# Two-layer transformer on one core: reordering square sums, scatters and one shared product in the first layer

## The reference

```python
def step(state, inp):                 # attention of layer 0: a scan with rotation, 6 heads of 64
    th, ps, ph, vt, at, bt = inp
    retained = _rotate(state, ph) * at[..., None]
    write = _rotate(vt, ps)
    new_state = retained + bt[..., None] * write
    out_t = _rotate(new_state, -th)
    return (new_state, out_t)
...
rms = jax.lax.rsqrt(jnp.mean(jnp.square(out), axis=-1, keepdims=True) + EPS)
o = out * rms * rms_w * jax.nn.silu(g)
return o.reshape(B, T, VALUE_DIM) @ Wo
...
shared = _swiglu(x, wg_s, wu_s, wd_s) * RATIO        # FFN of layer 0: shared part, 16 experts, 2 a token
affinity = jax.nn.sigmoid(jnp.einsum('bsh,eh->bse', x, centroids))
_, top_idx = jax.lax.top_k(affinity + gate_bias, K)
...
for e in range(E):
    routed = routed + mask[..., e:e + 1] * _swiglu(x, wg[e], wu[e], wd[e])
return shared + routed
```

## Time and profile before

| | us |
|---|---|
| median of three runs | 2143.7 |
| lowest, highest | 2142.53, 2146.38 |
| the profiled execution | 2146.1 |
| its span | 2144.4 |
| PE busy, share of the span | 2080.2 (97%) |
| DVE busy | 1641.0 (77%) |
| ACT busy | 1239.4 (58%) |
| POOL busy | 590.2 (28%) |

### The profile page before, as it was taken

One profiled execution on the slowest core, in us unless ns is written; L12 is line 12 of the kernel. 1 busy time (PEld: TensorE's weight loads), 2 busy tenths in 40 slices (PEclk: granted clock), 3 DMA queues, 4 the chain that ended last, 5 costly groups with the idle time before them and its releaser, 6 DMA issues. The chain is left out here.

```text
span 2144.4 us, 36740 instructions
## 1 busy us (share of the span) xinstructions
PE 2080.2 (97%) x12620; PEld 1809.7 (84%) x12620; DVE 1641.0 (77%) x4333; ACT 1239.4 (58%) x3432; POOL 590.2 (28%) x624
## 2 busy tenths in 40 slices
PE   6899999899999999999999999999999999999998
PEld 5777677577788999899899989988998999899887
DVE  6788787888878878768876777787687778767775
ACT  5443432236667666656665666666566666656662
POOL 3314354223133232223123311322231232112210
PEclk9999999999999999999999999999999999999999
DMA  6603021366422121113112211311221122111100
GB/s 193 205 1 104 33 77 48 150 191 199 144 74 60 45 75 55 40 43 97 40 41 71 68 40 40 91 43 44 66 70 40 40 79 60 40 50 45 41 20 20
DMA packets 92840, 154.56 MB, mean 72 GB/s; under 512 B 8688, under 2 KB 56560, under 8 KB 92656
## 3 DMA queue, kind: packets, MB, share of 16 engines
q1 hardware_dynamic: 72192, 121.53, 19.1%
q0 software_dynamic: 6144, 16.79, 2.4%
q10 hardware_dynamic: 14320, 13.90, 1.9%
HBM read 112.85 MB, written 39.32 MB: 71 GB/s over the span
## 5 line engine op out<-in xcount | busy, mean ns | idle before, releaser
L713 POOL TENSOR_TENSOR wo_low<-wraw_o,wo_high 128x256 fp32r<-128x256 f32 x128 | 95.1, 743 | 1141.2 <-ACT wo_high L777 1141.2
L1083 ACT ACTIVATE pr<-bank,negmax 128x128 f32<-128x128 f32 (+3 forms) x512 | 263.1, 527 | 195.4 <-DVE negmax L1645 195.4
L1203 DVE TENSOR_TENSOR p_low<-bank,p_high 128x512 fp32r<-128x512 f32 (+2 forms) x384 | 190.2, 551 | 101.5 <-ACT p_high L777 100.7
L777 ACT ACTIVATE p_high<-bank 128x512 fp32r<-128x512 f32 (+2 forms) x384 | 177.8, 497 | 149.6 <-PE bank L2208 149.6
L1645 DVE CUSTOM_DVE_ANT_0 bank<-bank,causal 128x128 f32<-128x128 f32 (+3 forms) x512 | 234.6, 520 | 1.1 <-PE bank L1832 1.1
L1672 DVE SCALAR_TENSOR_TENSOR xs<-bank,rinv,xs 128x256 f32<-128x256 f32 x512 | 211.7, 474 | 1.2 <-PE bank L1832 1.2
L1830 PE MATMUL bank<-h_high,wqk_high 128*128 128x512 f32 x512 | 202.6, 396 | 0.2 <-DVE h_low L1203 0.2
L1832 PE MATMUL bank<-h_high,wqk_low 128*128 128x512 f32 x512 | 202.5, 396 | 0.0
L1831 PE MATMUL bank<-h_low,wqk_high 128*128 128x512 f32 x512 | 202.4, 395 | 0.0
L1203 DVE TENSOR_TENSOR z_low<-bank,z_high 128x512 fp32r<-128x512 f32 x128 | 88.4, 691 | 130.8 <-ACT z_high L777 130.3
L703 POOL TENSOR_TENSOR wqk_low<-wraw,wqk_high 128x512 fp32r<-128x512 f32 x128 | 165.8, 1295 | 0.1
(11 more groups left out here) (349 smaller groups left out, 6185.8 us busy)
## 6 DMA issues: line engine op xcount, KB each, us to landing
wraw<-in_wpair SPq DMA_DIRECT2D x64, 512.0 KB, 4.0
wraw<-in_wpair SPq DMA_DIRECT2D x64, 256.0 KB, 4.3
wraw_o<-in_wpair SPq DMA_DIRECT2D x64, 256.0 KB, 2.9
tokens_by_expert<-xm SPq DMA_DIRECT2D x10, 1024.0 KB, 10.9
xt<-tokens_by_expert SPq DMA_DIRECT2D x40, 256.0 KB, 3.2
expert_results<-ey ACTq DMA_DIRECT2D x40, 256.0 KB, 3.7
wres<-in_wexp SPq DMA_DIRECT2D x1, 6144.0 KB, 19.7
xs<-x_between_stages SPq DMA_DIRECT2D x8, 512.0 KB, 4.9
```

The costliest lines, as they stand in the source:

```text
L713: pool.tensor_tensor(wo2[e][1][:], wraw_o[r][:, e, :], wo2[e][0][:].bitcast(F32), ALU.subtract).then_inc(s_wo, 1)
L777: sc.activation(dst, src, ACT.Copy, scale=scale).then_inc(done, 1)
L1083: ins = sc.activation(pr[:, i, 0:(i + 1) * P], score(i), ACT.Exp, scale=-1.0, bias=negmax[:, i:i + 1], accum_out=rsum[:, i:i + 1])
L1203: v.tensor_tensor(at(parts[1]), src, high_, ALU.subtract).then_inc(done, 1)
```

## The change

Three edits to the order of instructions; no instruction is added or removed, and none is computed otherwise.

1. In each pass, PE sums the squares of the third row ahead of both halves of the second row's value products. Before, it did so between the halves.
2. In passes 2 and 3, POOL issues all 16 scatters of unit y - 2 in one run, ahead of the three `beta_taken`. Behind the loop, the scatters of unit NU - 2 stay cut as before.
3. In the last pass, PE does the third gate/up pair ahead of the ranks, and DVE the first multiply ahead of the picks. The other passes keep their order.

```diff
@@ POOL
             for y in range(1, NU):
                 for r in range(RT):
                     gate_taken(y - 1, r)
+                if y >= 2:
+                    scatter(y - 2, 0, 2 * UT)
                 for r in range(RT):
-                    if y >= 2:
-                        scatter(y - 2, SCATTERS[r], SCATTERS[r + 1])
                     beta_taken(y, r)
@@ DVE, y + 1 == NU
                 else:
+                    shared_product(x, 0)
                     router_picks(x)
-                    shared_product(x, 0)
                     shared_product(x, 1)
                     places(x)
                     shared_product(x, 2)
@@ PE
                 square_sums(x, 1)
                 angle_products(y, 1)
-                value_products(y, 1, (0,))
                 square_sums(x, 2)
-                value_products(y, 1, (1,))
+                value_products(y, 1)
                 for r in range(RT):
                     rms_turn(x, r)
@@ PE, y + 1 == NU
                 else:
+                    shared_gate_up(x, 2)
                     router_ranks(x)
-                    shared_gate_up(x, 2)
                     shared_gate_up(x, 3)
                     for ab in range(2):
                         shared_down(x, ab)
```

More of the change, by code:

```diff
@@ L88 @@
 LATE_PART_HEAD = NH + 1
-SCATTERS = (0, 6, 11, 16)
+LAST_SCATTERS = (0, 6, 11, 16)
 NG = NB * NH
@@ L696, in _ @@
                 gate_taken(NU - 1, r)
-                scatter(NU - 2, SCATTERS[r], SCATTERS[r + 1])
+                scatter(NU - 2, LAST_SCATTERS[r], LAST_SCATTERS[r + 1])
             scatter(NU - 1, 0, 2 * UT)
```

## The result

| | kernel before | changed kernel |
|---|---|---|
| median of 20 runs each, us | 2143.43 | 2149.99 |
| lowest, highest | 2138.10, 2150.02 | 2146.66, 2155.40 |
| ratio of the times, 95% interval | | 1.0031 [1.0022, 1.0041] |

The change makes the kernel slower, by 4.7 to 8.8 us.

The account below looks back on a forecast made before the run. The prediction took TensorE to pace the kernel, so that idle time removed there is won. Its terms, 2.9 + 1.1 + 1.3 + 1.1 + 2.4 - 0.6 = 8.2 us won, gave 2136 us, range 2131 to 2141.5.

Parts of the forecast that it names:

- Square sums ahead of both value products: TensorE's waits for rexp in the loop: 2.9 us won in pass 1, 1.3 and 1.1 in passes 2 and 3.
- The clock behind that wait: Pass 1, rexp turns to next angle product: without the long wait the clock stays up, 1.1 us won.
- The third product: Pass 3: TensorE's 1.27 us wait for picks moves behind the ranks and grows, 0.6 us lost.
- Scatters in one run: Passes 2 and 3: last scatter lands some 7.5 us sooner, TensorE's wait for xm goes, 2.4 us won.
- The rival that came nearest: Passes 2 and 3: four multiplies hold VectorE's chain for 5.2 us, xm waits stay; 2138.5 us, chance 0.13.
- The slower rival: Third row's squares, three passes: coming 4.2 us later each, they delay both value products; 2148 us, chance 0.03.

Follow-up runs that it names:

- e1: Kernel before with only the third row's square sums moved ahead of both value products; 2141.20 us, ratio 0.9969.
- e4: Changed kernel with four beta multiplies (rows 0 and 1, passes 2 and 3) done on 8 of 512 columns; 2138.13 us, ratio 0.9959 to the kernel before.
- e10: Changed kernel with a tiny GpSimd memset and a wait for it between the 16 scatters and the multiplies; 2144.49 us, ratio 1.0002 to the kernel before.
- e9: Changed kernel with GpSimd waiting for its own end after each of the four beta multiplies; 2147.17 us, ratio 1.0017 to the kernel before.
- e2: Kernel before with only the 16 scatters of passes 2 and 3 put in one run, multiplies behind them; 2154.56 us, ratio 1.0038.
- e6: Kernel before with square sums ahead of both value products and the scatters cut 6 and 10; 2134.32 us, ratio 0.9957.
- e8: Kernel before with the changes of e6 and e7 together; 2133.67 us, ratio 0.9954.
- e5: Changed kernel with unread filler turns on TensorE ahead of the xm turns in passes 2 and 3; 2148.28 us, ratio 1.0019 to the kernel before.
- e7: Kernel before with the third gate/up pair ahead of the ranks, VectorE's first multiply ahead of picks and third ahead of places; 2143.46 us, ratio 0.9999.
- e3: Kernel before with only the third gate/up pair ahead of the ranks and VectorE's first multiply ahead of picks; 2145.70 us, ratio 1.0003.

## Why the prediction was wrong, step by step

- **Square sums ahead of both value products: right in mechanism, pass 1 too large.** In passes 2 and 3 the turns start 1.3 and 1.2 us sooner, counted from the start of the pass (forecast 1.3 and 1.1). In pass 1 only 1.4 sooner (forecast 2.9), though the wait of 3.22 us is gone altogether. Two things took the rest. I had let one step of DVE's chain be held beside the two multiplies by beta; in the changed kernel (1.23 and 1.22 us) and in e1 (1.29 and 1.22) it was two. My own figure for two holds was 1.9, and e1, where PEclk stays at 1.00, has 2.0, with 0.8 us of waiting left. And in the changed kernel the clock fell: the sums, short matmuls behind a 0.17 us wait, are followed by value products at a mean PEclk of 0.66 (96 to 101 us), so PE came to the turns too late to wait for them.
- **The clock behind that wait: right.** From the turns to the first xm turn pass 1 takes 1.2 us less (forecast 1.1). What I left out is the fall ahead of it.
- **The third product: right.** No wait for picks in the loop, 1.8 us at the first down product; alone it costs 0.5 us in the trace, and nothing that can be measured.
- **Scatters in one run: this is the step that failed.** Its times were right: pass 2 begins 4.3 us sooner than in the rows of before (1.8 of start, 2.6 of pass 1). Less these 4.3, the multiplies were forecast for 209.9 and stand at 209.95, and PE was to want xm at 218.1 and did so at 218.55 - 0.57 = 217.98. The factors were forecast for 212.4 to 213.8 and came at 216.32. "Between two multiplies one or two slip through" is what fell: none did. And "At most four steps of the chain are left by then" fell with it: the hold begins 0.68 us before the first multiply is shown, with eight steps to go, the held one among them. With 2.08 us for xm, that is 218.5, just too late for the first turn; and the second was not 0.2 but 1.7 us late, because each half of the chain takes 5.6 us and PE's work between the turns 3.7. So the waits for xm grew from 2.8 to 4.7 us, where I had them go.
- **The price of a wait was too small.** I counted waits of PE as their own length, except in pass 1. The new ones are 1.9 us longer in sum than the old, but the logits grew by 2.2 us in pass 2 and 2.0 us in pass 3. What follows them grew by 1.3 and 2.3 us more, at the lower clock too (mean PEclk 0.86 and 0.93), but that can't be put down to the waits: e4, with no wait for xm, takes 25.0 us for the last piece of pass 3 as well, and e1 20.5 for that of pass 2. The old wait, ahead of the first turn, had 2.8 us of value products and more behind it; the new one, ahead of the second turn, has the turn and the logits behind it.
- **The rival that came nearest** was the second, that POOL holds DVE for its whole 5.2 us, with a chance of 0.13. It named the place and the hold right, but said that PE would then wait as long as before, and priced it at 2138.5. It lacked both the second half and the clock. The slower rival, late squares, did not occur: the wait for them is 0.3 us in all.

A row of the kernel before already showed the hold, and I had not looked for it. Its last unit has two multiplies straight behind an indirect DMA; DVE first, then POOL:

```profile
369.25 0.69 DVE L1288 TENSOR_TENSOR tt<-tt 128x512 f32<-128x512 f32 x1
369.86 3.34 DVE L1289 TENSOR_TENSOR tt<-tt 128x512 f32<-128x512 f32 x1
```

```profile
369.16 0.96 POOL L643 DMA_INDIRECT tokens_by_expert<-xm,slots  x1 [0.30 <-issue]
370.14 1.28 POOL L625 TENSOR_TENSOR ge<-ge,oe 128x512 f32<-128x512 f32 x1
371.37 1.27 POOL L625 TENSOR_TENSOR go<-go,oo 128x512 f32<-128x512 f32 x1
```

An operation of 0.69 us takes 3.34, through both multiplies. The rows that I went by (rows 3 and 5) show a multiply that POOL starts after a wait of its own, 2.85 us for a DMA and 2.41 us for ACT: those let a step in at each change, as in e10. What differs between the two is what stood ahead of the multiplies on POOL, and edit 2 changes exactly that. The same step takes 3.33 to 3.35 us in the last unit of every profile of this study.

## What to carry to other kernels

When work on GpSimd is moved, look at what stands straight ahead of it and at the short VectorE steps beside it: multiplies behind an indirect DMA held one step through all four of them, and cutting the 16 scatters 6 and 10 so that the multiplies fell elsewhere turned +0.31% into -0.43% (without edit 3) or -0.46% (with it, mended). A producer that works in halves needs its slack for both: here 5.6 us a half against 3.7 us of cover, so the first half's lateness decides whether the second is late. And a wait of TensorE can cost more than its own length: here the short matmuls behind a wait of 1.7 us took 2 us longer at the lower clock.

## What the runs showed of the hardware

- **A hold longer than an instruction.** The Trainium skill (SBUF — State Buffer, Who interferes with whom) gives the shared ports to one of the two engines "for the whole instruction". Steps of 0.16 to 0.21 us that take 1.15 to 1.24 us beside one multiply agree with that (rows 3, rows 5, e10). Straight behind an indirect DMA the hold went through two multiplies (3.34 us) and through four (5.49, 5.61, 5.68, 5.69 us), which is longer than that. A 0.12 us operation with a wait behind it, put between, ended that (e10), and a wait between the multiplies cut it (e9). Why the indirect DMA matters isn't shown. The held step begins 0.28 to 0.69 us before the first multiply is shown to start, beside the last indirect DMA. Starting ahead of the multiply isn't enough: in e10 three steps begin 0.11 to 0.51 us before the first multiply, one beside the 0.12 us operation and two beside the DMA, and take 0.16 us each. It may be that the engines' claims were queued in some order that the trace doesn't show. No run here has a step with two inputs in SBUF that starts only after the first of such multiplies, so whether that one would be held through all of them isn't known.
- **A step with one tensor as input was held too.** e2's held step (L1222) reads one tensor of 128x4 and takes 5.49 us; in the kernel before one such step (L1186, pass 1) takes 0.93 us beside a multiply, where it takes 0.19 in the changed kernel. In e6 an add with one input in PSUM ran beside a multiply without delay (1.29 us for two, as elsewhere).
- **The clock differs between executions.** Its falls don't all come at the same places in two executions of near kernels: the kernel before has one at 107 to 112 us (rows 7), the changed kernel at 96 to 101. The last piece of pass 1 is 17.85 us in e6, e8, e9 and e10 (in e6 at a PEclk of 1.00), 19.4 to 19.6 in those of the kernel before, the changed kernel, e1, e4, e5 and e7 (0.91 in the first two and e4), and 20.6 in e2 and e3, with the same instructions in it. So a difference of 1 to 3 us in one piece of one pair of profiles proves nothing by itself.
- **What stays open** is how the loss of some 6.6 us divides between waits and clock. By the table, the one profile of the changed kernel loses 3.8 us up to the second turns, 4.2 in the logits and 3.6 behind them (0.5 of it edit 3) against 6.8 won elsewhere in the loop. e5, which filled the waits, got 2 to 3 back.
